# Weight low parts by accumulating DMA, and a re-ordered VectorE chain, in a cross-attention mask + mixture-of-experts kernel

## The reference, cut to what matters

```python
def xattn(h, adj, Wq, Wk, gamma_raw):        # h: context (4, 256, 64), adj: LayerNorm(x) (4, 256, 256)
    sim = (heads of h @ Wq.T) . (heads of h @ Wk.T), summed over 4 heads / (sqrt(d) * 4)
    threshold = top_k(sim, 76)[..., -1:]      # 76 = int(256 * 0.3)
    A = sigmoid(sim) * (sim >= threshold)
    A = (A + A.T) * 0.5
    return (1 - sigmoid(gamma_raw)) * adj + sigmoid(gamma_raw) * A

def ffn(x, gate_w, fc1_w, fc1_b, fc2_w, fc2_b, alpha):   # 8 experts, hidden 256, inner 256
    probs = softmax(x @ gate_w); score, idx = top_k(probs, 2); score /= sum(score)
    combine = one_hot(idx) weighted by score, times alpha
    return sum over e of combine[:, e] * (gelu(x @ fc1_w[e] + fc1_b[e]) @ fc2_w[e] + fc2_b[e])

x = x + xattn(ctx, layernorm(x), ...)
x = x + ffn(layernorm(x), ...)
```

## Time and profile before

| | us |
|---|---|
| median of 3 runs | 138.14 (137.96 to 138.16) |
| the profiled execution | 137.94 |
| its span in the trace | 136.2 |
| outside the span | 1.7 |
| first `up(0)` matmul starts | 24.23 |
| TensorE busy / VectorE / ScalarE / GpSimd | 121.4 / 102.3 / 83.4 / 72.2 |

### The profile page before, as it was taken

The page is one execution under the profiler, slowest core; times in us unless marked ns, Lnnn a source line. Parts: engine busy times, 40 slices in busy tenths (PEclk is TensorE's granted clock), DMA queues, the critical chain, the costliest instruction groups (busy, mean ns, idle before and its releaser), DMA issues.

```text
span 136.2 us, 2763 instructions
## 1 busy us (share of the span) xinstructions
PE 121.4 (89%) x904; PEld 110.5 (81%) x904; DVE 102.3 (75%) x401; ACT 83.4 (61%) x207; POOL 72.2 (53%) x69
## 2 busy tenths in 40 slices
PE   6796989999429998999879999996999999999990
PEld 4433756899339988999779999995999999999990
DVE  0078898989999819899997879999976526943472
ACT  3188789799055746865399487663954645445620
POOL 2046656989908997565029735430594334454300
PEclk9999999999986999999999999999999999999999
DMA  2999940000000000001100000020000002000002
GB/s 63 218 397 415 413 162 0 0 5 2 0 0 0 5 0 0 2 0 44 38 2 2 0 5 0 2 77 2 5 0 0 5 0 77 0 0 5 2 0 77
DMA packets 2516, 6.90 MB, mean 51 GB/s; under 512 B 300, under 2 KB 772, under 8 KB 2500
## 3 DMA queue, kind: packets, MB, share of 16 engines
q1 hardware_dynamic: 2500, 6.71, 13.8%
HBM read 5.66 MB, written 1.05 MB: 49 GB/s over the span
## 4 chain that ended last, share of the span: by engine, by line
PE 49%; DVE 32%; issue 6%; POOL 6%; ACT 4%; DVEq 0%; POOLq 0%
PE p_y L473 21%; PE p_h L451 19%; DVE acc L1054 7%; DVE picked L1011 4%; POOL w_lo L660 3%; DVE left L873 3%; DVE above L835 2%; PE p_y L354 2%; DVE left L884 2%; ACT h_act L568 2%; DVE comb L1016 1%; DVE weight L1014 1%; POOL rstd L649 1%; PE p_a L378 1%; DVE guess L829 1%
## 5 line engine op out<-in xcount | busy, mean ns | idle before, releaser
L681 POOL TENSOR_TENSOR h_lo<-h_act,h_hi 128x512 fp32r<-128x512 f32 x31 | 40.7, 1317 | 43.9 <-ACT h_hi L576 28.9
L568 ACT ACTIVATE h_act<-p_h,small_sb 128x256 f32<-128x256 f32 x64 | 26.7, 469 | 20.1 <-PE p_h L451 19.8
L451 PE MATMUL p_h<-xt_hi,w_hi 128*128 128x256 f32 x128 | 33.2, 282 | 0.1
L451 PE MATMUL p_h<-xt_hi,w_lo 128*128 128x256 f32 x128 | 33.0, 280 | 0.0
L473 PE MATMUL p_y<-w_hi,h_hi 128*128 128x256 f32 x126 | 26.4, 291 | 6.9 <-DVE acc L1054 6.9
L1054 DVE SCALAR_TENSOR_TENSOR acc<-p_y,comb,acc 128x256 f32<-128x256 f32 x55 | 24.0, 476 | 11.3 <-PE p_y L473 10.2
L473 PEld LDWEIGHTS p_y<-w_hi,h_hi 128*128 128x128 f32 x126 | 19.4, 191 | 7.6 <-issue 7.4
L451 PE MATMUL p_h<-xt_lo,w_hi 128*128 128x256 f32 x128 | 25.5, 280 | 0.0
L473 PE MATMUL p_y<-w_lo,h_hi 128*128 128x256 f32 x126 | 25.4, 284 | 0.0
L473 PE MATMUL p_y<-w_hi,h_lo 128*128 128x256 f32 x126 | 25.4, 284 | 0.0
L451 PEld LDWEIGHTS p_h<-xt_hi,w_hi 128*128 128x128 f32 x128 | 24.4, 191 | 0.4 <-issue 0.4
(11 more groups left out here) (140 smaller groups left out, 182.9 us busy)
## 6 DMA issues: line engine op xcount, KB each, us to landing
w_sb<-w SPq DMA_DIRECT2D x8, 512.0 KB, 8.0
x_sb<-x SPq DMA_DIRECT2D x1, 768.0 KB, 8.3
out<-acc SPq DMA_DIRECT2D x3, 256.0 KB, 2.5
x_sb<-x SPq DMA_DIRECT2D x1, 256.0 KB, 4.6
out<-acc SPq DMA_DIRECT2D x2, 128.0 KB, 2.0
attn_sb<-attn SPq DMA_DIRECT2D x1, 192.0 KB, 5.0
small_sb<-small SPq DMA_DIRECT2D x1, 97.5 KB, 4.6
attn_sb<-attn SPq DMA_DIRECT2D x1, 96.0 KB, 2.3
```

Of the source, the lines that this page charges most:

```text
L451: last = nc.tensor.matmul(dst, w_[:, e, 0, k, c * P:(c + 1) * P], v[:, b % 2, k, :], start=n == 0, stop=n == len(trio) - 1)
L568: last = nc.scalar.activation(h_act[:, s % 2, c], tiled(p_h[s % 2])[:, c, :], ACT.Gelu, bias=b1_sb[:, e, c:c + 1])
L681: nc.gpsimd.tensor_tensor(h_lo[:, s % (LAG + 1)], h_act[:, s % 2], h_hi[:, s % (LAG + 1)], ALU.subtract).then_inc(h_lo_ready, 1)
```

## The change

**Low parts by accumulating DMA.** For experts 2 to 7 ScalarE writes `-w_hi` into `w_lo` (`weight_neg`, one pass over 128 x 1024), and a DMA issued by GpSimd adds the weights from HBM to it (`weight_rest`, 512 KB each). `up(s)` waits for that DMA (`w_rest_in`) and `down(s)` for nothing more. GpSimd computes only the four halves of experts 0 and 1. GpSimd now makes `w_hi` of 0, 2, 1, 6, 7 (in that order), ScalarE of 3, 4, 5. VectorE makes none of the low parts.

**VectorE in front.** `gamma_terms` moves to the start (`small` is loaded before the rest of the context), `ln1_affine(0)` goes to GpSimd, `ln1(1)` moves from before `residual(0)` to step 1, `flag_few` and `flag_missed` work on both tiles at once, `flag_missed` comes behind `drop_above`. The offset and guess of tile 1 are interleaved with the count of tile 0.

**The gate's picks and sums** are written to PSUM in place of SBUF; their sum becomes a `tensor_reduce`. `best_f` is copied in four single columns.

**GpSimd held:** it waits for `base_sum` (the masked sum) before `weight_hi(1)`, where it waited for `masked` before two `weight_lo`.

**Later batches:** `guesses(b+2)` moves from step 7 to 5, `middle_guess` from step 0 of the next batch to 7, `better_guess`, counts and `drop_above` from step 1 to 0, `drop_eight` from 2 to 1; ScalarE's spreads and signs move one step or more forward. `base(1)` goes from step 2 to 3. `keep_warm` issues 12 and 5 in place of 18 and 3.

```diff
-POOL_HI = 2
+POOL_HI = (0, 2, 1, 6, 7)
+ACT_HI = (3, 4, 5)
+POOL_HI_AT = {0: 6, 2: 7}
-WARM_BEFORE_XN = 18
-DVE_SPLITS = (6, 7)
+WARM_BEFORE_XN = 12
...
+        PICKED = p_g[:, at:at + TILES * 2 * EXPERTS].rearrange("p (t j e) -> p t j e", t=TILES, j=2)
+        WEIGHT = p_g[:, at:at + TILES * EXPERTS].rearrange("p (t e) -> p t e", t=TILES)
...
+            sp.dma_start(small_sb[:], small).then_inc(small_in, 16)
             sp.dma_start(attn_sb[:, first:], attn[:, first:]).then_inc(ctx_in, 16)
-            sp.dma_start(small_sb[:], small).then_inc(small_in, 16)
...                                            # up(s)
-                    pe.wait_ge(w_lo_ready[e][0], 1)
+                    if e < 2:
+                        pe.wait_ge(w_lo_ready[e][0], 1)
+                    else:
+                        pe.wait_ge(w_rest_in[e], 16)
...                                            # down(s)
-                if b == 0:
+                if b == 0 and e < 2:
                     pe.wait_ge(w_lo_ready[e][1], 1)
...                                            # ScalarE
+            def weight_neg(e):
+                if e in POOL_HI:
+                    act.wait_ge(w_hi_early, POOL_HI.index(e) + 1)
+                else:
+                    act.wait_ge(w_hi_ready, ACT_HI.index(e) + 1)
+                nc.scalar.activation(w_lo[:, e], w_hi[:, e], ACT.Copy, scale=-1.0).then_inc(w_neg_ready, 1)
...                                            # ScalarE in front of the steps
             sigmoid(0)
-            weight_hi(POOL_HI)
-            for b in range(1, BATCHES):
+            weight_hi(3)
+            sim_copy(1)
+            spread_of(1)
+            weight_neg(2)
+            weight_neg(3)
+            for b in range(2, BATCHES):
                 sim_copy(b)
-            weight_hi(POOL_HI + 1)
-            spread_of(1)
-            weight_hi(POOL_HI + 2)
-            weight_hi(POOL_HI + 3)
+            weight_hi(4)
             signs_of(1)
             xt_hi_of(0)
             signs_again_of(1)
+            weight_hi(5)
...                                            # ScalarE in the steps
+                if s < 2:
+                    weight_neg(4 + s)
+                if s in (1, 3):
+                    weight_neg(6 + s // 2)
+                if s == 3:
+                    base(1)
...                                            # GpSimd
+            def weight_rest(e):
+                pool.wait_ge(w_neg_ready, e - 1)
+                nc.gpsimd.dma_start(w_lo[:, e], w[:, e].bitcast(F32R), accum_op=ALU.add).then_inc(w_rest_in[e], 16)
...
             weight_lo(0, 0)
-            weight_hi(1)
+            ln1_affine(0)
             base(0)
-            weight_lo(1, 0)
...                                            # gate_parts low
-            pool.wait_ge(masked, TILES)
-            weight_lo(0, 1)
-            weight_lo(2, 0)
+            weight_hi(2)
+            pool.wait_ge(base_sum, 1)
+            weight_hi(1)
             rstd(veps2, rstd2, 0, ln2_veps, ln2_rstd)
             pool.wait_ge(xn_ready, TILES)
-            weight_lo(3, 0)
+            weight_rest(2)
+            weight_lo(1, 0)
+            weight_lo(0, 1)
+            weight_rest(3)
             weight_lo(1, 1)
-            weight_lo(4, 0)
...                                            # in the steps: hidden_lo(s), then
-                if s == 0:
+                if s == 1:
                     rstd(veps1, rstd1, 1, ln1_veps, ln1_rstd)
-                    weight_lo(2, 1)
+                if s < 4:
+                    weight_rest(4 + s)
+                if s in POOL_HI_AT:
+                    weight_hi(POOL_HI_AT[s])
...                                            # VectorE
-                        step(nc.vector.tensor_scalar(picked[:, t, r], iota_sb, best_f[:, t, r:r + 1],
+                        step(nc.vector.tensor_scalar(PICKED[:, t, r], iota_sb, best_f[:, t, r:r + 1],
                                                      score[:, t, r:r + 1], ALU.is_equal, ALU.mult))
-                step(nc.vector.tensor_tensor(weight[:], picked[:, :, 0], picked[:, :, 1], ALU.add))
+                step(nc.vector.tensor_reduce(WEIGHT, PICKED.rearrange("p t j e -> p t e j"), AX.X, ALU.add))
...
+                nc.vector.tensor_scalar(few[:], count[:], TOP_K - WINDOW, None, ALU.is_lt).then_inc(few_ready, 1)
...
+                nc.vector.scalar_tensor_tensor(missed[:], count[:], TOP_K, few[:], ALU.is_ge,
+                                               ALU.add).then_inc(missed_ready, 1)
```

More of the change, by code:

```diff
@@ L208, in xattn_moe_program @@
         u_ready = sem("u_ready")
+        w_neg_ready = sem("w_neg_ready")
+        w_rest_in = [sem(f"w_rest_in{e}") for e in range(EXPERTS)]
         rows_cleared = sem("rows_cleared")
@@ L653, in weight_hi @@
                 nc.gpsimd.tensor_copy(w_hi[:, e], w_sb[:, e]).then_inc(w_hi_early, 1)
+            def weight_rest(e):
+                pool.wait_ge(w_neg_ready, e - 1)
+                nc.gpsimd.dma_start(w_lo[:, e], w[:, e].bitcast(F32R), accum_op=ALU.add).then_inc(w_rest_in[e], 16)
             def weight_lo(e, j):
[L656 to L659, removed]
+                pool.wait_ge(w_hi_early, POOL_HI.index(e) + 1)
                 nc.gpsimd.tensor_tensor(w_lo[:, e, j], w_sb[:, e, j], w_hi[:, e, j],
@@ L669, in base, with ln1_affine @@
                 last.then_inc(base_ready, 1)
+            def ln1_affine(b):
+                pool.wait_ge(gam_ready, 1)
+                pool.wait_ge(ln1_agg, (b + 1) * TILES)
+                pool.wait_ge(ln1_rstd, b + 1)
+                for t in range(TILES):
+                    nc.gpsimd.tensor_scalar(mul1[:, b, t:t + 1], rstd1[:, b, t:t + 1], gam[:, 2:3], ones[:], ALU.mult,
+                                            ALU.add)
+                    last = nc.gpsimd.tensor_scalar(add1[:, b, t:t + 1], mv1[:, b, t, 0:1], gam[:, 3:4],
+                                                   rstd1[:, b, t:t + 1], ALU.mult, ALU.mult)
+                last.then_inc(ln1_mul, 1)
             def add_masked(b):
@@ L831, in better_guess @@
                                         ALU.subtract).then_inc(better_ready, 1)
+            def better_guess(b, t):
+                offset_again(b, t)
+                second_guess(b, t)
             def count_above(b, t):
@@ L838, in flag_few @@
             def flag_few(b):
[L840 to L843, removed]
+                dve.wait_ge(counted, (b + 1) * TILES)
+                nc.vector.tensor_scalar(few[:], count[:], TOP_K - WINDOW, None, ALU.is_lt).then_inc(few_ready, 1)
             def flag_missed(b):
@@ L848, in flag_missed @@
                     dve.wait_ge(missed_sum, b)
-                for t in range(TILES):
-                    dve.wait_ge(few_ready, b * TILES + t + 1)
-                    nc.vector.tensor_scalar(missed[:, t:t + 1], count[:, t:t + 1], TOP_K, few[:, t:t + 1],
-                                            ALU.is_ge, ALU.add).then_inc(missed_ready, 1)
+                dve.wait_ge(few_ready, b + 1)
+                nc.vector.scalar_tensor_tensor(missed[:], count[:], TOP_K, few[:], ALU.is_ge,
+                                               ALU.add).then_inc(missed_ready, 1)
             steps = [0]
@@ L996, in top2 @@
                 settle()
-                step(nc.vector.tensor_copy(best_f[:], best_at[:, :, 0:2]))
+                for t in range(TILES):
+                    for r in range(2):
+                        step(nc.vector.tensor_copy(best_f[:, t, r:r + 1], best_at[:, t, r:r + 1]))
             def combine(b):
@@ L1066, in _ @@
             nc.vector.memset(warm[:], 1.0).then_inc(warm_set, 1)
+            gamma_terms()
             for t in range(1, TILES):
@@ L1079, in _ @@
                 middle_guess(0, t)
-            for t in range(TILES):
-                better_guess(0, t)
-                count_above(0, t)
-            flag_few(0)
-            gamma_terms()
+            offset_again(0, 0)
+            second_guess(0, 0)
+            offset_again(0, 1)
+            count_above(0, 0)
+            second_guess(0, 1)
+            count_above(0, 1)
             drop_above(0)
-            ln1_affine(0)
             take_eight(0)
@@ L1094, in _ @@
             add_masked(0)
-            ln1(1)
             residual(0)
@@ L1106, in _ @@
                 more = nxt < BATCHES
-                if more and b and e == 0:
-                    for t in range(TILES):
-                        middle_guess(nxt, t)
-                if more and e == (1 if b else 0):
+                if more and e == 0:
                     for t in range(TILES):
@@ L1116, in _ @@
                     drop_above(nxt)
-                if b < BATCHES and e == (2 if b else 0):
-                    top2(b)
+                if s == 0:
+                    top2(0)
                 if more and e == 1:
@@ L1121, in _ @@
                 if s == 1:
+                    ln1(1)
                     combine(0)
+                if more and e == 1:
```

(18 more changed lines are left out.)

52 lines of the change are left out of this document (22 added, 30 removed).

## The result

The changed kernel takes 134.79 us (median of 4, 134.68 to 135.25) against 138.15 us (137.96 to 138.24) run beside it: a ratio of 0.9765, 95% interval 0.974 to 0.979. It is faster by 3.4 us where 7.9 were forecast; the time lies in the range, at the place of rival A, but by coincidence: the trace shows that A's mechanism had little part in it. The profiled execution has a span of 132.9 us (136.2 before), so 3.3 us are to be found.

A forecast was written before the change was run, and what follows sets the result against it. TensorE was taken as the bound, winnable only before `up(0)`, in gaps and at low clock. 4.7 + 0.9 + 2.3 = 7.9 off 137.94 gave 130.0, median 130.2; range 127.4 to 135.2 us.

The forecast's parts named there:

- rival A: Accumulating transfers land late, 8.0 us with 1.28 per issue; `up(7)` at 49.1, nothing won there; 134.9 us, chance 0.18.
- The front: Before `up(0)`: work leaves VectorE's chain, so `up(0)` starts at 22.5 in place of 24.2, 1.7 us won.
- The gate: Batch 0's picks and sums in PSUM cost 0.87 + 0.2 + 0.2 in place of 6.7; 5.4 us leave VectorE.
- Rival E: Batch 0's picks wait in PSUM too, `add_expert(0)` done near 40; 133 us, chance 0.04.
- I = 1.04 and L = 4.3: Accumulating DMA: GpSimd's time in us for one `weight_rest`, and the time from its end to landing.
- part 3: GpSimd and accumulating DMAs in batch 0: `up(7)` at 44.5, before 49.17; 4.7 us won, the front's 1.7 included.
- The last sentence of the prediction: Wrong if an issue exceeds 2, a landing 8.0, or VectorE is late in batch 0, through flags or `ln1_affine(1)`.
- Rival C: VectorE keeps waiting for the port, one 1.28 pass each; batches 1 and 2 lose 1.3 each; 132.6 us, chance 0.10.
- Rival D: TensorE's gaps between `up(2)` and `up(5)` bring 1.2 GHz, 1.3 us lost; 131.5; chance inside the forecast's 0.60.
- Rival B: GpSimd is slow at issuing its six DMAs; at 3 us each `up(7)` starts at 55.7; 141.4 us, chance 0.08.
- Batches 1 and 2: VectorE's chain from `xt_lo` to `add_expert` shortens, closing TensorE's gaps of 1.40 and 1.2; 2.3 us won.
- The gap of 0.9 before `xn`: TensorE's gap between `up(7)` and batch 1's transposes goes as GpSimd does `rstd` in time; 0.9 us won.

The follow-up runs named there:

- the kernel of 130.7 us: The changed kernel with one edit: GpSimd waits for batch 1's flags before `weight_lo(1, 1)`; 130.70 us, ratio 0.9471.
- the three self-waits: The changed kernel with GpSimd waiting for its own weight pass before `hidden_lo` of steps 0, 1 and 3; median 133.17 us.
- the late `h_hi(0)`: Seen in the changed kernel with `ln1(1)` in front of batch 1's better guess (step 0), not in step 1; 133.78 us, ratio 0.9694.
- the plain-copy kernel: The changed kernel, its six DMAs copying the weights into `w_lo` without adding (another result); median 132.39 us, four runs from 129.93 to 133.76.

## Why the prediction was right or wrong

**The front: right**, 1.43 for 1.7. `xn` began at 21.11 (22.54 before) and `ln1_affine` on GpSimd took 1.3 us under cover.

**The gate: right in mechanism and price.** The picks in PSUM are free, 0.86 for four. The Trainium skill, "SBUF — State Buffer", section "Who interferes with whom", has it that a VectorE instruction with at most one SBUF input, outside the two-port modes, doesn't contend with GpSimd; the trace agrees. I charged 5.4 us off VectorE, and alone the part is worth 3.5 of time. Rival E (the picks wait in PSUM too) is out by that.

**GpSimd and the DMA: sizes nearly right.** I took I = 1.04 and L = 4.3; they were 1.13 and 4.8. Expert 5's DMA comes, without the hold-up, at 32.80 to my 32.8, and `up(5)` at 38.77 to my 38.2: the kernel of 130.7 us does what part 3 says. Some of that agreement is luck: GpSimd began its run at 22.27, not at 21.6, and was 0.7 faster over it than I charged. That kernel wins 7.3 of the 7.9 forecast. What the part misses is the credit: "this decides" holds for the bound on `up(7)`, but the gate alone brought `up(7)` to 45.54. By its sum the landing decides at `up(5)`; the waits of 0.51 and 0.70 there agree. Rival A's 8 us didn't come (5.7 to 6.3 from issue), so that the measured time lies where A put it is a coincidence.

**The step that failed** is the sentence in part 3 that takes `ln1_affine(1)` as waiting for GpSimd only, with `add_expert(0)` done by 35. It was done at 40.0. VectorE's own work in steps 0 and 1 was charged at its free durations: the hold was a term of nothing in the sum, and it measured 6.71 us for two `left` that take 0.42 each when free. I had named the hold in rival C, but sized it by a row of the kernel before, one pass of 1.28 in each of batches 1 and 2, and placed it there, at 132.6. It came in batch 0, 6.7 us long. Behind it lay not `add_expert` but two things that the change itself had moved there: `flag_missed`, put behind both `left`, with TensorE's `sum_missed` waiting for it in front of `down(0)`; and `ln1(1)`, put behind `take_eight` in step 1, with GpSimd's `rstd` and expert 5's DMA behind it. The kernel before had the flags in front of the second `left` and `ln1(1)` in front of both. The price, 4.1 us, is what one added wait gives back; 7.9 - 4.1 = 3.8 is close to the 3.4 measured. The last sentence of the prediction names this way of being wrong (VectorE late in batch 0, through the flags), but no price stood beside it.

**Rival C** had the right instruction type and the right edit under suspicion (`few`, held 0.98). It erred in the premise, drawn from the earlier trace rows, that VectorE gets a turn between any two passes: here one `left` was held past two passes and an issue, and the next past two passes.

**Rival D** didn't come true as it was put. A low clock came, but behind the gap of 3.44; in the kernel of 130.7 us the short waits for DMAs stand (0.51 and 0.70) and the granted clock is 1.000. **Rival B** didn't either: six issues of 1.13.

**Batches 1 and 2: right.** Both gaps are gone and 2.3 us were won from the transposes on, for 2.3 forecast. **The gap of 0.9 before `xn`** went as well: 1.00 - 0.07 = 0.9. No run takes the front or the later batches away by themselves; their prices are read from the traces before and after.

## What to carry to other kernels

A VectorE instruction with two SBUF inputs beside GpSimd can be held past several of GpSimd's passes, not one: here up to the whole run (6.56 and 4.75 us). Look in the trace for passes whose records overlap behind a DMA issue; that sign failed once here. Where VectorE has a few such instructions on the critical path, one semaphore wait on GpSimd in front of its next pass cost GpSimd 0.1 us here and gave back 4.1. Ask too which of several changes a gain belongs to: the gate's few lines gave as much as the whole change. When a wait has two heirs (here TensorE's own gap and a late DMA), taking away one shows nothing: undo the cause, not the symptom.

## What the runs showed of the hardware that was not expected

- Behind a DMA issue, GpSimd's following passes are often listed from before the last one's end, and VectorE then misses its turn at that boundary: `left` 4.32 and 2.47 us (6.56 with the picks in SBUF), `missed` 2.91, `chosen` 2.54, `comb` 4.75. Where the passes follow without an issue, or can't stand ready behind each other, it gets in at each boundary: picks at 1.07 each, `chosen` at 1.33, two `left` at 3.62 and at 1.84. That a pass standing ready behind an issue is the reason is what the three self-waits and the late `h_hi(0)` speak for; the plain-copy kernel has one hold past two passes (2.96) and one turn between two (1.48) that it doesn't explain, so how VectorE's turn is granted stays open.
- An accumulating DMA of 512 KB took 5.9 us from issue to landing, the same copy without adding 4.4, and its issue occupied GpSimd for 1.13 us against 0.58.
- Two of these kernels spread by 2.5 and 3.8 us over four runs, the others by 0.01 to 1.2. Why was not tried.
